# Five layers of message passing on a graph: one product's buffer doubled, its sums cut in two around a gather, and one addition placed earlier on VectorE

## The chip, the cores and the metric

The kernel runs on one core of one Trainium2 chip. The metric is the device time of one execution in microseconds (us), median of several runs; lower is better.

## What is computed

The graph has 12,500 nodes of 64 features and 200,000 edges of 32 features, sorted by their destination. The reference, cut to what matters:

```python
h = jnp.maximum(_layernorm(x), 0.0)
for l in range(5):
    h_ = _leaky(x @ W1[l] + b1[l]) @ W2[l] + b2[l]
    e = _leaky(edge_attr @ We1[l] + be1[l]) @ We2[l] + be2[l]
    msg = h_[src] * e * dot_scale[l]
    agg = jax.ops.segment_sum(msg, dst, num_segments=n)
    out = x + agg * res_w[l]
    x = layernorm(out) * ln_g[l] + ln_b[l]
return x_input + x
```

(Inside the loop `x` is the state that starts as `h`.)

## The kernel before

All values are 32-bit floats. The state of all nodes lies in SBUF, features on partitions 0 to 63 (`nodes_state`). The rows `h_[src]` come from a table in HBM (`h_rows`) that each layer writes. The edges are split in two kinds.

**Slot edges.** The first 101,376 edges in the order of the destinations, in 9 chunks, were sorted by source in a prologue into 126 groups of 1,024 slots, 14 per chunk, so that the 112 source rows of a group are contiguous in the table. They are loaded by plain DMAs and spread to the slots by a product with a one-hot matrix (`gathered`, line 1053). **Window edges.** The other 97 groups of 1,024 edges have their source rows gathered by indirect DMAs on GpSimd (line 793), 8 per group, into a ring of 9 buffers; one more group holds the spilled edges of the chunks. 92 of these 98 groups are spread over the 126 steps of a layer's loop (so about three steps in four have one; `a_at(s)` is None in the others), and 6 follow in six tail steps.

One loop step `s` works on three groups at different depths. The order on each engine is written out by hand in `step` and is this (in brackets: only where that step has a window group, or where a tile of nodes is due):

- TensorE: [hidden layer of window group s+2], hidden layer of slot group s+2 (line 976), [second layer of window group s+1], second layer of slot group s+1 (line 980), [window sums of s, line 1016], **chunk sums** of s (`chunk_sums`, line 1029: 32 products of 64x64 by 64 x width in four quadrants of the array), [a part of a node tile, "middle"], the slot gather of s+1 (line 1053), [a part of a node tile, "end"].
- VectorE: [window product of s: gathered rows times edge values, line 1750], **slot product** of s (line 1757), [one-hot matrix of the next window group, line 1670, 640 elements], leaky ReLU of s+2 for both kinds (line 1662), bias of the slot edges of s+1 then of the window edges of s+1 (line 1666), ["middle"], the **one-hot matrix of the slots** of s+1 (line 1670, 8 x width elements), [**window additions**: two additions of the window sums of s into the state, line 1718, with two register loads of their column, line 1782], [at a chunk's end: four additions of the chunk's sums, line 1731, with two register loads of their own, line 1724], ["end"].
- ScalarE: a tenth of the hidden values of s+2 (line 1241), and parts of node tiles.

The chunk's width is the number of destination columns: 360, 328, 288, 248, 208, 168, 128, 88 and 48 in the nine chunks. Hidden values and sums of window groups share one PSUM bank (`win_ps` is `hid_ps[0]`). So TensorE's hidden layer of s+3 waits in step s+1 until all additions of step s are done (`added`, in `step` of TensorE). The second layer of window group s+1 overwrites `e_ps`, so it waits for the window product of s; the second layer of the slots waits for the slot product, the gather for the slots' bias. There is one buffer for slot products, so the slot product of s waits until the chunk sums of s-1 are done (`sum_ready`). When the sums of all nodes of a tile are final, the tile's normalization and the next layer's node network are done in fixed places of nine steps in a row: centering and variance on TensorE at the "end" of the first two, reciprocal (line 1604) in the "middle" of the third step on VectorE. The variance also uses the shared bank and waits for the same step's window additions. Up to twelve places for tiles lie in the loop, two in the six tail steps; the rest of the tiles follows.

## Time and profile before

| what | value |
|---|---|
| median of 3 runs | 6610.09 us (6605.63 to 6611.65) |
| the profiled execution | 6615.82 us |
| span of its profile | 6614.0 us |
| TensorE matmul busy | 5622.6 us, 85% of the span |
| VectorE busy | 5148.4 us, 78% |
| GpSimd busy | 4527.2 us, 68% |
| ScalarE busy | 1133.9 us, 17% |
| moved by DMA | 886.20 MB, 134 GB/s in the mean |

The first 1,250 us are the sorting prologue. Then come five layers. In each the 126 steps take about 980 us (from the first slot product to the last: 987.2, 984.0, 979.4, 987.7 and 941.7 us), and the tail, the remaining nodes and the start of the next layer about 105 us. An engine's busy share is a mean over steps in which another one may be the limit; so the waits inside a step say more. In lists of waits "A <- B: us, times, longest" means that A's queue stood still until B had finished. A wait on "issue" is time in which the profile shows nothing that the engine waited for: its sequencer was busy with register loads or branches, which are no busy time.

### The profile page before, as it was taken

Reading aid. Unit: us, or ns where it says so; the run is one execution under the profiler, and the core shown is the slowest. Engines: PE = TensorE matmul, PEld = TensorE weight load, DVE = VectorE, ACT = ScalarE, POOL = GpSimd, SP = SyncE. Lnnn points to the kernel's source line nnn. Section 1 sums busy time; section 2 is a strip of 40 time slices with the busy share of each in tenths; the row PEclk is TensorE's granted clock in tenths of the full one; section 3 lists DMA queues with packets and bytes.
Section 4 is the critical chain, followed back from the end, with each engine's and each line's share of the span. In section 5 each row is a group of like instructions: output and inputs, shape, how many; then the busy total and the mean of one; then the engine's idle time right before and its main releaser. Section 6 shows DMA issues by size and latency. Waiting matters only on the chain.

```text
span 6614.0 us, 169076 instructions
## 1 busy us (share of the span) xinstructions
PE 5622.6 (85%) x63332; PEld 3676.7 (56%) x63333; DVE 5148.4 (78%) x7991; ACT 1133.9 (17%) x1726; POOL 4527.2 (68%) x4793
## 2 busy tenths in 40 slices
PE   6776899988888788888878888888898887888887
PEld 2223444456666555666655666655566665556665
DVE  8997544688887688888768888867888875888886
ACT  0000211111122211112211112221111222111111
POOL 5777777666677377777727777746777773777775
PEclk9997555799999799999979999988999997999998
DMA  3112399755566355656635655644565563666664
GB/s 135 26 26 47 78 240 242 185 131 138 138 148 152 96 132 136 142 141 154 159 80 133 145 143 143 162 112 116 129 147 142 148 161 78 139 147 156 151 171 110
DMA packets 733545, 886.20 MB, mean 134 GB/s; under 512 B 325488, under 2 KB 502976, under 8 KB 731568
## 3 DMA queue, kind: packets, MB, share of 16 engines
q1 hardware_dynamic: 568480, 703.64, 40.8%
q0 software_dynamic: 152144, 154.93, 12.4%
q10 hardware_dynamic: 12096, 16.53, 0.8%
q8 instruction: 530, 8.68, 0.6%
q14 instruction: 295, 2.42, 0.1%
HBM read 749.51 MB, written 125.06 MB: 132 GB/s over the span
## 4 chain that ended last, share of the span: by engine, by line
PE 54%; DVE 21%; issue 15%; DVEq 4%; ACT 3%; DMA 1%; POOL 0%; ACTq 0%; SPq 0%; POOLq 0%
PE bank L980 14%; PE bank L976 8%; PE bank L1029 7%; PE bank L1053 5%; PE bank L922 4%; PE bank L879 3%; DVE arena L1662 3%; PE bank L1016 3%; PE bank L860 2%; PE bank L845 2%; DVEq L1782 2%; DVE arena L1750 2%; ACT arena L1241 2%; DVE arena L1670 2%; DVE arena L1408 2%
## 5 line engine op out<-in xcount | busy, mean ns | idle before, releaser
L793 POOL DMA_INDIRECT arena<-h_rows,src x3855 | 3674.3, 953 | 1693.5 <-issue 1250.7
L980 PEld LDWEIGHTS bank<-w2s,arena 128*128 128x128 f32 x8960 | 1175.7, 210 | 772.3 <-DVE arena L1750 437.2
L980 PE MATMUL bank<-w2s,arena 128*128 128x128 f32 x8960 | 1307.0, 303 | 208.2 <-DVE arena L1750 191.4
L780 POOL DMA_INDIRECT slots<-arena,slot_index x792 | 787.2, 994 | 267.2 <-issue 241.3
L976 PE MATMUL bank<-nodes_state,edge_w 64*128 64x512 f32 x980 | 598.4, 693 | 307.3 <-DVE nodes_state L1718 142.6
L1053 PEld LDWEIGHTS bank<-arena 112*64 112x64 f32 x20160 | 640.4, 138 | 267.0 <-issue 245.1
L1053 PE MATMUL bank<-arena 112*64 112x64 f32 x20160 | 725.8, 225 | 60.1 <-issue 54.2
L976 PE MATMUL bank<-x_packed,edge_w 64*128 64x512 f32 x1260 | 740.1, 669 | 16.4 <-ACT std L1190 15.6
L1241 ACT ACTIVATE arena<-bank,tenth 128x512 f32<-128x512 f32 x490 | 335.5, 685 | 2296.6 <-PE bank L976 2296.6
L1662 DVE SCALAR_TENSOR_TENSOR arena<-bank,edge_w,arena 128x512 f32<-128x512 f32 x490 | 366.7, 748 | 424.1 <-ACT arena L1241 421.4
L1670 DVE TENSOR_TENSOR x_packed<-bank,slot_rel 128x2880 f32<-128x2880 f32 (+8 forms) x315 | 588.9, 1870 | 15.8 <-issue 15.8
L1670 DVE TENSOR_TENSOR arena<-bank,slot_rel 128x2880 f32<-128x2880 f32 (+8 forms) x315 | 588.6, 1869 | 12.5 <-issue 12.5
L1666 DVE TENSOR_TENSOR arena<-bank,b2s 128x512 f32<-128x512 f32 x630 | 432.4, 686 | 157.4 <-PE bank L980 153.7
L1241 ACT ACTIVATE x_packed<-bank,tenth 128x512 f32<-128x512 f32 x630 | 430.0, 683 | 680.0 <-PE bank L976 680.0
L1029 PE MATMUL bank<-x_packed,arena 64*64 64x288 f32 (+8 forms) x10080 | 524.3, 346 | 0.0
L1029 PE MATMUL bank<-arena 64*64 64x288 f32 (+8 forms) x10080 | 523.9, 346 | 0.0
L1662 DVE SCALAR_TENSOR_TENSOR arena<-bank,edge_w,x_packed 128x512 f32<-128x512 f32 x630 | 467.6, 742 | 59.5 <-ACT x_packed L1241 51.7
L1757 DVE TENSOR_TENSOR arena<-arena,bank 128x512 f32<-128x512 f32 x630 | 429.4, 682 | 43.8 <-PE bank L1053 39.1
L1016 PE MATMUL bank<-arena 128*64 128x80 f32 x7760 | 411.3, 253 | 42.4 <-DVE arena L1662 35.4
L1016 PEld LDWEIGHTS bank<-arena 128*64 128x64 f32 x7760 | 328.4, 148 | 122.3 <-DVE arena L1662 60.4
L1670 DVE TENSOR_TENSOR arena<-bank,rel 128x640 f32<-128x640 f32 x485 | 396.1, 817 | 0.0
L1029 PEld LDWEIGHTS bank<-x_packed,arena 64*64 64x64 f32 x10080 | 311.1, 135 | 127.8 <-issue 6.5
(198 smaller groups left out, 5615.6 us busy)
## 6 DMA issues: line engine op xcount, KB each, us to landing
arena<-slot_pick SPq DMA_DIRECT2D x630, 448.0 KB
arena<-h_rows SPq DMA_DIRECT2D x630, 224.0 KB
x_packed<-slot_attr SPq DMA_DIRECT2D x630, 128.0 KB
nodes_state<-attr_t SPq DMA_DIRECT2D x485, 128.0 KB
arena<-h_rows,src POOLq DMA_INDIRECT x3855
slot_pick<-arena SPq DMA_DIRECT2D x126, 448.0 KB
x_packed<-slots SPq DMA_DIRECT2D x127, 136.0 KB, 4.9
slots<-arena SPq DMA_DIRECT2D x9, 1904.0 KB, 22.1
```

The lines of the kernel that those rows point to most:

```text
L780: pool.indirect_dma_start(slots, bass.IndirectOffsetOnAxis(ap=slot_index[:, t:t + 1], axis=0), records[:, v, j, :], None).then_inc(record_ ...
L793: pool.indirect_dma_start(to[0:n, at:at + D], None, table, bass.IndirectOffsetOnAxis(ap=index[0:n, t:t + 1], axis=0)).then_inc(landed(t), 16)
L976: return pe.matmul(hid_ps[k][:, :], edge_w[rows_of, 0:P], attributes, start=True, stop=True)
L980: mm = pe.matmul(to[:, j * P:(j + 1) * P], acts[:, j * TILE:(j + 1) * TILE], w2s[:, :], start=True, stop=True)
L1016: mm = pe.matmul(win_ps[side * D:(side + 1) * D, 0:WIN], msg[:, 0, at:at + D], pick[:, k % 2, side * TPH + j, :], start=(j == 0), stop=(j ...
L1029: mm = pe.matmul(sum_ps[half][side * D:(side + 1) * D, 0:w], msg[slots_of, 1, at:at + D], slot_places[i % 2][slots_of, k * w:(k + 1) * w], ...
L1053: mm = pe.matmul(slot_ps[half * D:(half + 1) * D, k * D:(k + 1) * D], source_pick[0:ROWS, i % 2, slot:slot + D], source_rows[0:ROWS, i % 2 ...
L1241: return act.activation(hid_tenth[k], hid_ps[k][:, :], ACT.Identity, scale=SLOPE, bias=tenth[:, :])
L1662: return dve.scalar_tensor_tensor(out, hid_ps[k][:, :], edge_w[:, 2 * P + D:2 * P + D + 1], hid_tenth[k], ALU.add, ALU.max)
L1666: return dve.tensor_tensor(out.rearrange("p (t f) -> p t f", f=D), of.rearrange("p (t f) -> p t f", f=D), b2s[:, :].unsqueeze(1).to_broadc ...
L1670: return dve.tensor_tensor(out, column_ps[:, 0:n].unsqueeze(1).to_broadcast((P, tiles, n)), where.unsqueeze(2).to_broadcast((P, tiles, n)) ...
L1757: dve.tensor_tensor(msg[:, 1, :], slot_e, slot_ps[:, :], ALU.mult).then_inc(slot_msg_ready, 1)
```

## The change

Three things are changed.

1. The slot products get two buffers, taken in turn (`slot_msg`). The second lies in a free part of `x_packed`. The wait ahead of the slot product goes; a wait for the chunk sums of an earlier group stands now ahead of the slots' one-hot matrix.
2. The chunk sums are made in two calls of 16 products each: the first stands where all 32 stood, the second behind the slot gather. The products with the spilled edges at a chunk's end follow the second.
3. On VectorE the window additions with their register loads stand ahead of the "middle" part and ahead of the slots' one-hot matrix. The chunk's additions keep their place at the end.

```diff
+        slot_msg = [msg[:, 1, :], late["msg"]]
...
-                def chunk_sums(i):
+                def chunk_sums(i, begin, end):
...
-                    for j in range(TPH):
+                    for j in range(begin, end):
...
-                                mm = pe.matmul(sum_ps[half][side * D:(side + 1) * D, 0:w], msg[slots_of, 1, at:at + D],
+                                mm = pe.matmul(sum_ps[half][side * D:(side + 1) * D, 0:w], slot_msg[i % 2][slots_of, at:at + D],
...
-                    if ends_chunk(i):
+                    if ends_chunk(i) and end == TPH:
...
-                        chunk_sums(s)
+                        chunk_sums(s, 0, TPH // 2)
                     part("middle")
                     if k is not None:
                         pe.wait_ge(slot_e_biased, l * NB + k + 1)
                         gathered(k)
+                    if b_at(s) is not None:
+                        chunk_sums(s, TPH // 2, TPH)
...
-                        if i > 0:
-                            dve.wait_ge(sum_ready, 4 * (l * (NB + CHUNKS) + i + i // BG))
-                        dve.tensor_tensor(msg[:, 1, :], slot_e, slot_ps[:, :], ALU.mult).then_inc(slot_msg_ready, 1)
+                        dve.tensor_tensor(slot_msg[i % 2], slot_e, slot_ps[:, :], ALU.mult).then_inc(slot_msg_ready, 1)
...
+                    if k is not None and k != SPILL_AT:
+                        group = GB0 + real(k)
+                        window_start[:] = [dve.value_load(start_i[0:1, 2 * group + side:2 * group + side + 1],
+                                                          min_val=0, max_val=NPAD) for side in range(2)]
+                        window_added(s, k)
                     part("middle")
                     if i is not None:
                         w = widths[i // BG]
+                        if i > 1:
+                            dve.wait_ge(sum_ready, 4 * (l * (NB + CHUNKS) + i - 1 + (i - 1) // BG))
                         one_hot(slot_places[i % 2][:, 0:TPG * w].rearrange("p (t w) -> p t w", w=w), TPG, w,
                                 slot_rel[:, i * TPG:(i + 1) * TPG])
...
-                    if k is not None and k != SPILL_AT:
-                        group = GB0 + real(k)
-                        window_start[:] = [dve.value_load(start_i[0:1, 2 * group + side:2 * group + side + 1],
-                                                          min_val=0, max_val=NPAD) for side in range(2)]
-                        window_added(s, k)
                     if ends_chunk(s):
                         chunk_added(s)
```

What this does to the order of VectorE at a chunk's end (the first chunk, width 360; the next chunk's width is 328, so the slots' one-hot matrix has 2624 elements). TENSOR_LOAD is a register load, ISA and REGISTER_ALU are waits and register arithmetic. Before:

```order
L1666 TENSOR_TENSOR arena<-bank,b2s 128x512
L1670 TENSOR_TENSOR arena<-bank,slot_rel 128x2624
L1782 TENSOR_LOAD start_i
L1782 ISA x2
L1782 TENSOR_LOAD start_i
L1782 ISA x2
L1714 ISA
L1716 REGISTER_ALU
L1718 ISA
L1718 TENSOR_TENSOR nodes_state<-nodes_state,bank 64x80
L1716 REGISTER_ALU
```

After the second window addition come the chunk's two register loads and additions at once. In the changed kernel:

```order
L1669 TENSOR_TENSOR arena<-bank,b2s 128x512
L1774 TENSOR_LOAD start_i
L1774 ISA x2
L1774 TENSOR_LOAD start_i
L1774 ISA x2
...
L1721 TENSOR_TENSOR nodes_state<-nodes_state,bank 64x80
L1781 ISA
L1673 TENSOR_TENSOR arena<-bank,slot_rel 128x2624
L1727 TENSOR_LOAD chunk_start
L1727 ISA x2
L1727 TENSOR_LOAD chunk_start
```

The window's register loads and additions moved ahead of the one-hot matrix, and the matrix stands now between them and the chunk's register loads.

The same for TensorE in a step of the third chunk (width 288) that has a part of a node tile in its "middle" (line 860 before, 861 after). Before:

```order
L1016 MATMUL bank<-arena 64x80 x8
L1029 MATMUL bank<-arena 64x288 x16
L461 COMPARE_AND_BRANCH
L1128 ISA
L857 REGISTER_ALU
L860 MATMUL bank<-node_w,y_act 112x64 x8
L461 UNCONDITIONAL_BRANCH
L1053 MATMUL bank<-arena 64x64 x16
```

In the changed kernel:

```order
L1017 MATMUL bank<-arena 64x80 x8
L1030 MATMUL bank<-arena 64x288 x8
L462 COMPARE_AND_BRANCH
L1131 ISA
L858 REGISTER_ALU
L861 MATMUL bank<-node_w,y_act 112x64 x8
L462 UNCONDITIONAL_BRANCH
L1054 MATMUL bank<-arena 64x64 x16
L1030 MATMUL bank<-arena 64x288 x8
```

Half of the chunk sums (the program's count; in the profile each such product shows twice) stands behind the gather now. No instruction is added but one wait, and one goes.

## Rows read from the trace of the kernel before

**Rows 1.** The page: busy time, share of the span, instructions, by engine.

```profile
PE 5622.6 (85%) x63332; PEld 3676.7 (56%) x63333; DVE 5148.4 (78%) x7991; ACT 1133.9 (17%) x1726; POOL 4527.2 (68%) x4793
```

**Rows 2.** Third layer: us; busy PE, PEld, DVE, ACT, POOL; clock; DMA; GB/s.

```profile
3428.40:3541.00 112.60, 100.73 (x1296) 64.93 (x1296) 102.49 (x126) 14.15 (x22) 85.43 (x90) 0.98 0.62 141
...
4331.00:4407.80 76.80, 68.82 (x1145) 53.57 (x1145) 58.89 (x104) 16.02 (x24) 50.17 (x53) 0.96 0.65 164
...
4407.80:4513.40 105.60, 72.57 (x338) 45.22 (x338) 46.56 (x73) 22.78 (x35) 12.84 (x14) 0.58 0.15 39
```

**Rows 3.** Waits of the whole run: who waited for whom, us, times, longest.

```profile
DVE arena L1662 <- ACT arena L1241: 421.4, 346, 8.5
...
PE bank L980 <- DVE arena L1750: 191.4, 172, 3.5
...
PE bank L976 <- DVE nodes_state L1718: 142.6, 138, 4.8
```

**Rows 4.** VectorE in time, first chunk: start, duration, instruction, count, [idle before <- releaser].

```profile
3459.81 0.68 DVE L1750 TENSOR_TENSOR arena<-arena,bank 128x512 f32<-128x512 f32 x1
...
3461.00 0.81 DVE L1670 TENSOR_TENSOR arena<-bank,rel 128x640 f32<-128x640 f32 x1
...
3463.65 0.69 DVE L1666 TENSOR_TENSOR bank<-bank,b2s 128x512 f32<-128x512 f32 x1
3464.25 3.14 DVE L1670 TENSOR_TENSOR x_packed<-bank,slot_rel 128x2880 f32<-128x2880 f32 x1
3467.31 0.59 DVE L1718 TENSOR_TENSOR nodes_state<-nodes_state,bank 64x80 f32 x2
3467.93 0.69 DVE L1750 TENSOR_TENSOR arena<-arena,bank 128x512 f32<-128x512 f32 x1
...
3475.65 0.69 DVE L1750 TENSOR_TENSOR arena<-arena,bank 128x512 f32<-128x512 f32 x1
...
3506.23 0.69 DVE L1750 TENSOR_TENSOR arena<-arena,bank 128x512 f32<-128x512 f32 x1
...
3508.29 0.75 DVE L1662 SCALAR_TENSOR_TENSOR arena<-bank,edge_w,arena 128x512 f32<-128x512 f32 x1 [0.78 <-ACT arena L1241]
...
3513.90 0.69 DVE L1757 TENSOR_TENSOR arena<-arena,bank 128x512 f32<-128x512 f32 x1
...
3521.63 0.67 DVE L1750 TENSOR_TENSOR arena<-arena,bank 128x512 f32<-128x512 f32 x1
```

**Rows 5.** TensorE in time: two rows of the last chunk, three of the first.

```profile
3259.72 0.78 PE L1016 MATMUL bank<-arena 128*64 128x80 f32 x16
...
3260.42 0.68 PE L1029 MATMUL bank<-x_packed,arena 64*64 64x48 f32 x32
...
3463.23 2.65 PE L1029 MATMUL bank<-arena 64*64 64x360 f32 x32
3465.81 1.15 PE L1053 MATMUL bank<-arena 112*64 112x64 f32 x32
...
3514.11 0.66 PE L976 MATMUL bank<-nodes_state,edge_w 64*128 64x512 f32 x1 [0.58 <-DVE nodes_state L1718]
```

**Rows 6.** VectorE in time, last chunk: window additions behind a short one-hot matrix.

```profile
3272.07 0.56 DVE L1670 TENSOR_TENSOR arena<-bank,slot_rel 128x384 f32<-128x384 f32 x1 [0.45 <-issue]
...
3273.62 0.60 DVE L1718 TENSOR_TENSOR nodes_state<-nodes_state,bank 64x80 f32 x2 [0.99 <-issue]
```

**Rows 7.** Chunk's ends: what line 1731 waited for, and TensorE after one.

```profile
  issue: 42.9, 35
...
3034.20 1.19 PE L976 MATMUL bank<-nodes_state,edge_w 64*128 64x512 f32 x1 [5.66 <-DVE nodes_state L1731]
```

**Rows 8.** Line 838 (variance of a node tile, TensorE): what it waited for, us, times.

```profile
  DVE nodes_state L1718: 19.1, 36
```

**Rows 9.** TensorE in the tail: first product of the next layer's node network.

```profile
3349.56 1.11 PE L845 MATMUL bank<-nodes_state,node_w 64*128 x1 [4.25 <-ACT nodes_state L1275]
```

**Rows 10.** GpSimd in time: a layer's first gather, with the idle time before it.

```profile
3411.86 0.95 POOL L793 DMA_INDIRECT arena<-h_rows,src  x1 [100.66 <-issue]
```

More of the change, by code:

```diff
@@ L170, in build @@
         late, at = {}, 0
-        for name, n in dict(place=TPG * WMAX, tenth=HALF, attr=2 * HALF, x=TN, spill_pick=WMAX, spill_msg=HALF).items():
+        for name, n in dict(place=TPG * WMAX, tenth=HALF, attr=2 * HALF, x=TN, spill_pick=WMAX, spill_msg=HALF, msg=HALF).items():
             late[name] = x_packed[:, at:at + n]
```

## The prediction

> **What bounds the kernel now.** I read the page first, then stretches by chunk, then the list of waits, then single steps in time. By the page [rows 1] TensorE is busy 85% and VectorE 78%; neither is full. The stretches [rows 2] show why: in the widest chunk both are nearly full (TensorE 100.73 and VectorE 102.49 of 112.60 us), in the narrowest TensorE leads (68.82 against 58.89 of 76.80), and the tail is a chain in which nobody is full. So a step is set by the two engines handing work to each other, and the reader should look at the waits between them [rows 3]: VectorE stands 421.4 us before a leaky ReLU until ScalarE has its tenth, which only means that TensorE's hidden layer came late; TensorE stands 142.6 us before the hidden layer for the window additions, and 191.4 us before the second layer for the window product. A wait in one of these lists can be covered by the other engine's work, so I walk a few steps.
>
> A step of the widest chunk with all its parts runs on VectorE without a gap: window product to window product 8.12 us (3459.81 to 3467.93) [rows 4]. The next takes 7.72 us (to 3475.65). Where the following group is missing it takes 7.67 us (3506.23 to 3513.90), with 0.78 us idle before the leaky ReLU at 3508.29; and where its own window group is missing 7.73 us (3513.90 to 3521.63), although it has the least work. A turn of four steps with three window groups is therefore about 8.12 + 7.72 + 7.67 + 7.73 = 31.24 us. The idle time comes from TensorE's hidden layer, which starts only when the window additions are over: 0.58 us idle at 3514.11 [rows 5]. The additions stand behind a one-hot matrix of 3.06 us (start to next start) [rows 4]. That is the cycle which the change opens.
>
> **Part 1, the additions earlier.** They run now right behind the bias. The hidden layer then never waits for them in a wide chunk: TensorE has the chunk sums of 2.58 us (3463.23 to 3465.81) and the gather of 1.15 us [rows 5] to do before it gets there. What does not change is that the window product follows the one-hot matrix, and that the second layer waits for it; that wait (191.4 us) stays.
>
> What is new is the register loads. Where nothing covers them, the additions start 1.55 us after the instruction that went out before them: 3272.07 to 3273.62, 0.99 us of it idle [rows 6]. Before, the long one-hot matrix hid them. Now only the two biases of 0.60 us each stand ahead, and all leave together when the slots' second layer ends. So the exposed time is 1.55 - 1.20 = 0.3 us with both biases, 1.55 - 0.60 = 0.9 us with one, less what VectorE still has queued. The Trainium skill (Runtime: NRT & Kernel Launch, Instruction fetch mechanics) puts a register load at about 200 ns, so two would hide behind one bias and the 0.3 and 0.9 would be zero; by that the four-step turn below would gain another 0.95 us, some 50 us over the three widest chunks. Our row shows more, so I keep the row's price.
>
> The four steps again, by what each instruction takes of VectorE from its start to the next start: 0.60 us for a bias or a product, which is 0.09 under its duration; by the same measure 0.66 for a leaky ReLU and 0.73 for the small one-hot matrix (0.75 and 0.81 long); 3.06 for the slots' matrix and 0.62 for the two additions [rows 4]. All parts: 8.12, unchanged, since VectorE is some 0.6 us behind TensorE at the bias and that hides the loads. No window leaky ReLU: VectorE is on time at the bias, so the exposed 0.3 us shows, 8.12 - 0.66 + 0.3 = 7.8. No following window group, so neither small matrix nor second bias: 8.12 - 0.73 - 0.60 + 0.65 (0.9 less a backlog of 0.25) = 7.45. No own window group, so neither product, additions nor loads: 8.12 - 0.60 - 0.62 = 6.9. Together 30.3 against 31.24 us, or 0.23 us a step. Bounds: 0 (every exposure lands and the hidden layer's gain is eaten by the second layer's wait) to 0.4. I take 0.2 for the three widest chunks, 42 steps x 5 layers x 0.2 = **-42 us**; half for the next three, where one-hot matrix and chunk sums shrink alike but the exposure does not, **-21 us**; none for the last three.
>
> **Part 1 at a chunk's end.** Before, the chunk's register loads followed the additions directly: 42.9 us idle in 35 places [rows 7]. Now the one-hot matrix stands between and hides them. TensorE stands in front of the chunk's additions there (5.66 us in one case), so this is on the path. Most of it, **-35 us** (bounds -43 and -15, as the window's loads may be exposed instead).
>
> **Part 1 at node tiles.** The variance waited 19.1 us for window additions [rows 8]. Half of it, **-10 us** (bounds -19 and 0), since TensorE then waits for ScalarE's root in the same place. The reciprocal, 2.94 us, now stands behind the additions; in the loop it delays only the window product, as before. In the tail it is different: there TensorE's next hidden layer stands behind the first product of the node network, which waits (4.25 us) for the normalized tile [rows 9]. Additions and their loads push the tile back by 0.62 + 0.9 less what the reciprocal waited anyway: about 1.4 us, twice in each of four layers, **+11 us** (bounds 0 and 13).
>
> **Part 2, the sums in two halves.** Nothing is added to TensorE's work. The gather comes earlier by half the chunk sums, 1.3 us at width 360 and 0.3 us at 48 [rows 5]. Its cover while the slots' bias runs (0.67 us with its start) shrinks by the same. With window sums ahead (0.70 us, 3259.72 to 3260.42) that is enough. In a step without them the narrow chunks leave 0.3 to 0.65 us of cover: a stall up to 0.35 us in 27% of the 56 steps of four chunks in five layers is 76 x 0.35 = 27 us at most; the second half then covers VectorE, so I take **+10 us** (bounds 0 and 27). The hidden layer stands where it stood counted from the second layer, and the slot product is not among the long waits [rows 3], so an earlier gather gains nothing by itself. Next late is the window product.
>
> **Part 3, the second buffer.** The removed wait was always met, because the old sums were done before the gather on the same queue; 0. The new wait asks for sums two groups back; 0. Without the second buffer the slot product would have to wait for the second half: the buffer pays for part 2.
>
> Sum: -42 - 21 - 35 - 10 + 11 + 10 = -87 us. The profiled execution took 6615.8 us (span 6614.0, the rest around it), 5.7 above the median; I subtract from the median 6610.1: **6523 us**, given as 6520.
>
> **Rivals.**
> - *The register loads set the pace; slower.* Place: VectorE between bias and window additions, in every loop step with a window group: 91 a layer, 455 in all, 170 of them with one bias. Full price 170 x 0.9 + 285 x 0.3 = 239 us, against it the 142.6 us of the hidden layer's waits, the chunk's ends and the other terms (-35 - 10 + 21): about +72 us, **6680 us**. It decides when VectorE arrives at the bias without a backlog in most steps. For it: in the narrow chunks TensorE leads. Against: in the wide ones VectorE is the one behind.
> - *A wash.* The hidden layer's wait moves to the second layer's, and only the ends of chunks (-35), tiles (-10) and the costs (+21) stay: -24, and part of that lost, **6590 to 6610 us**.
> - *The clock.* After the 5.66 us gap TensorE's products took 1.19 us where the same took 0.66 at 3514.11 [rows 5, 7], so it had fallen from 2.4 to 1.2 GHz; the granted clock of the loops is 0.96 to 0.98 [rows 2], or 4 to 8% of the five loops' 4880 us at the lower level, about 300 us, in which half is lost. If shorter gaps keep it up half the time, another -75 us: **6445 us**. The Trainium skill (TensorE: Matmul & The Clock Gate, Part 1: The HAM clock gate) says that activity releases the throttle and idling sets it, which would favour this; the gap shrinks by a quarter only, so I doubt it.
> - *GpSimd.* It ends its gathers 100.66 us before the next layer's first one [rows 10], so it bounds nothing unless a layer's loop loses well over 60 us.
>
> That the change doesn't do what it says is no rival: the order shows the moves.
>
> **How the numbers follow.** My forecast (6520, own range 6480 to 6565) has 0.50; the clock 0.13; the wash 0.14; the register loads 0.20; something else 0.03. About 0.2% (13 us) is what a measurement can tell from no change. Faster: 0.50 + 0.13 + a part of the wash 0.05 = 0.68; same: 0.10; slower: 0.22. The range leaves out about half of the clock's case below and half of the slower case above: 6440 to 6680.
>
> **What would show it.** Right: the hidden layer's wait for line 1721 (was 1718) falls from 142.6 us to under 40; VectorE's wait before the leaky ReLU from 421 to under 350; "issue" before the chunk's additions from 42.9 to near 0, while "issue" before the window additions rises by 50 us or more; the first chunk of a layer falls from 112.6 us [rows 2] by about 3. Wrong: TensorE's wait for the window product above 300 us, or the gather waiting for the bias by more than 60 us, with the loop no shorter.

## The result and the profile after

| | before | after |
|---|---|---|
| median | 6610.87 us, 4 runs (6605.63 to 6620.89) | **6656.53 us**, 4 runs (6649.67 to 6663.22) |
| the profiled execution; its span | 6615.82; 6614.0 us | 6649.67; 6647.8 us |

The ratio is 1.0065, with a 95% interval of 1.0049 to 1.0081. So the change costs 46 us, where 87 us were to be gained: the sign of the forecast is wrong.

The page of the kernel after, busy time by engine, to be held against [rows 1]:

```profile
PE 5676.3 (85%) x63332; PEld 3617.7 (54%) x63333; DVE 5173.4 (78%) x7991; ACT 1136.4 (17%) x1726; POOL 4520.1 (68%) x4793
```

TensorE issues the same 63,332 products and is busy 53.7 us longer. The page's groups say where (columns: line, engine, operation, tiles, count, busy us, mean ns, idle before with its releaser). The chunk sums, line 1030 now:

```profile
L1030 PE MATMUL bank<-x_packed 64*64 64x288 f32 (+8 forms) x10080 | 597.0, 353 | 0.0
L1030 PE MATMUL bank<-arena 64*64 64x288 f32 (+8 forms) x10080 | 594.4, 351 | 0.0
...
L1721 DVE TENSOR_TENSOR nodes_state<-nodes_state,bank 64x80 f32 x970 | 227.4, 234 | 266.5 <-PE bank L1017 101.5
```

and the same lines of the kernel before:

```profile
L1029 PE MATMUL bank<-x_packed,arena 64*64 64x288 f32 (+8 forms) x10080 | 524.3, 346 | 0.0
L1029 PE MATMUL bank<-arena 64*64 64x288 f32 (+8 forms) x10080 | 523.9, 346 | 0.0
```

The same 20,160 products take 1191.4 us of busy time instead of 1048.2: 143 us more, although the mean of one product has hardly moved (353 and 351 ns against 346). A busy time counts overlapping products once; it grew because less of the stretch overlaps. Why is to be seen in single steps. TensorE in time, a step of the widest chunk, kernel after (start, us, line, tiles, count):

```profile
3467.01 0.77 PE L1017 MATMUL bank<-arena 128*64 128x80 f32 x16
3467.71 1.44 PE L1030 MATMUL bank<-arena 64*64 64x360 f32 x16
3469.08 1.15 PE L1054 MATMUL bank<-arena 112*64 112x64 f32 x32
3470.16 1.44 PE L1030 MATMUL bank<-arena 64*64 64x360 f32 x16
3471.53 1.12 PE L977 MATMUL bank<-x_packed,edge_w 64*128 64x512 f32 x2
```

and a step of the narrowest one:

```profile
3262.26 0.45 PE L1030 MATMUL bank<-x_packed 64*64 64x48 f32 x16
3262.64 1.15 PE L1054 MATMUL bank<-arena 112*64 112x64 f32 x32
3263.72 0.45 PE L1030 MATMUL bank<-x_packed 64*64 64x48 f32 x16
3264.10 1.12 PE L977 MATMUL bank<-x_packed,edge_w 64*128 64x512 f32 x2
```

Read the starts, not the durations. At width 360 the first half takes 3469.08 - 3467.71 = 1.37 us and the second 3471.53 - 3470.16 = 1.37, together 2.74; the whole took 2.58 in [rows 5]. At width 48 the halves take 0.38 each, together 0.76; the whole took 0.61 (3260.42 to the gather at 3261.03). The difference is nearly the same, 0.15 to 0.16 us, at a width that is 7.5 times smaller. So it is no work of the products but a fixed cost of each unbroken stretch of chunk sums, and the split makes two stretches of one. The medians over the steps at the full granted clock say the same:

| width | whole, 32 products | half, 16 products | two halves less the whole |
|---|---|---|---|
| 360 | 2.581 us | 1.371 | 0.161 |
| 208 | 1.568 | 0.864 | 0.160 |
| 128 | 1.034 | 0.598 | 0.162 |
| 88 | 0.767 | 0.464 | 0.161 |
| 48 | 0.612 | 0.378 | 0.144 |

With 0.155 us in each of the 126 steps of five layers, 630 steps, this is **98 us** of TensorE. (A layer's last step has no gather to split around; the 625 others with the medians of the table give 99 us.) I call it the run-out below; whether it is paid at the start or at the end of a stretch, the rows do not say. In the sums of line 1030 above, each stretch is also drawn 0.07 us longer than its start-to-start time; a second stretch adds that once more, 44 us, and 98 + 44 = 142 is the 143 us that these groups grew by. The gather itself takes 1.08 us to the next start in both kernels, whether the hidden layer or a half of the sums follows.

The third layer by stages, kernel after, for [rows 2] (us; busy PE, PEld, DVE, ACT, POOL; clock; DMA; GB/s); the second row covers the same twelve steps as there:

```profile
3432.30:3544.35 112.05, 101.47 (x1296) 62.77 (x1296) 102.71 (x126) 14.13 (x22) 84.75 (x90) 0.98 0.58 143
4347.60:4427.65 80.05, 70.29 (x1146) 54.25 (x1145) 60.04 (x104) 16.02 (x24) 45.84 (x49) 0.98 0.59 156
4427.65:4531.35 103.70, 66.92 (x338) 42.47 (x336) 46.69 (x74) 22.76 (x35) 12.19 (x13) 0.62 0.14 40
```

The widest chunk is 0.55 us shorter, where 3 us were expected, the narrowest is 3.25 us longer than its 76.80, and the tail is 1.9 us shorter.

The waits of the kernel after (who waited for whom, us, times, longest), against [rows 3]:

```profile
DVE arena L1665 <- ACT arena L1244: 327.4, 239, 8.3
...
PE bank L981 <- DVE arena L1753: 265.3, 199, 4.8
...
DVE nodes_state L1721 <- PE bank L1017: 101.5, 112, 4.0
DVE nodes_state L1721 <- issue: 88.8, 243, 1.1
...
PE bank L1054 <- DVE arena L1669: 27.1, 61, 1.0
...
PE bank L977 <- DVE nodes_state L1721: 2.8, 6, 1.0
```

The hidden layer's wait for the window additions is gone (142.6 to 2.8 us), as planned; the second layer's wait for the window product (now line 1753) went from 191.4 to 265.3, and VectorE stands 190 us ahead of the window additions (101.5 + 88.8), where it stood 64.5 (62.9 on issue and 1.6 for the window sums).

### The profile page after: what moved, and what is told of

Its sections match the earlier page's. It is cut to its first block, busy times and chain, and to the rows that moved or that the text cites. A ratio compares the mean times of both kernels' runs of the same rounds, so it can differ in the third digit from the quotient of the medians.

```text
span 6647.8 us, 169040 instructions
## 1 busy us (share of the span) xinstructions
PE 5676.3 (85%) x63332; PEld 3617.7 (54%) x63333; DVE 5173.4 (78%) x7991; ACT 1136.4 (17%) x1726; POOL 4520.1 (68%) x4793
## 4 chain that ended last, share of the span: by engine, by line
PE 54%; DVE 22%; issue 16%; DVEq 3%; ACT 3%; DMA 1%; POOL 0%; ACTq 0%; SPq 0%; POOLq 0%
PE bank L981 13%; PE bank L1030 8%; PE bank L977 6%; PE bank L1054 6%; PE bank L923 4%; DVE arena L1665 4%; PE bank L1017 3%; PE bank L880 3%; PE bank L846 2%; DVE arena L1753 2%; PE bank L861 2%; DVE arena L1411 2%; PE bank L902 2%; DVE arena L1669 2%; DVEq L1774 2%
## 5 line engine op out<-in xcount | busy, mean ns | idle before, releaser
L981 PEld LDWEIGHTS bank<-w2s,arena 128*128 128x128 f32 x8960 | 1160.3, 208 | 879.4 <-DVE arena L1753 518.2
L981 PE MATMUL bank<-w2s,arena 128*128 128x128 f32 x8960 | 1293.7, 300 | 324.9 <-DVE arena L1753 265.3
L1665 DVE SCALAR_TENSOR_TENSOR arena<-bank,edge_w,arena 128x512 f32<-128x512 f32 x490 | 366.4, 748 | 335.9 <-ACT arena L1244 327.4
L1030 PE MATMUL bank<-x_packed 64*64 64x288 f32 (+8 forms) x10080 | 597.0, 353 | 0.0
L1030 PE MATMUL bank<-arena 64*64 64x288 f32 (+8 forms) x10080 | 594.4, 351 | 0.0
L1721 DVE TENSOR_TENSOR nodes_state<-nodes_state,bank 64x80 f32 x970 | 227.4, 234 | 266.5 <-PE bank L1017 101.5
L1669 DVE TENSOR_TENSOR bank<-bank,b2s 128x512 f32<-128x512 f32 x490 | 338.5, 691 | 31.8 <-PE bank L981 31.7
```

What stands on the lines that cost most here:

```text
L981: mm = pe.matmul(to[:, j * P:(j + 1) * P], acts[:, j * TILE:(j + 1) * TILE], w2s[:, :], start=True, stop=True)
L1030: mm = pe.matmul(sum_ps[half][side * D:(side + 1) * D, 0:w], slot_msg[i % 2][slots_of, at:at + D], slot_places[i % 2][slots_of, k * w:(k + ...
L1665: return dve.scalar_tensor_tensor(out, hid_ps[k][:, :], edge_w[:, 2 * P + D:2 * P + D + 1], hid_tenth[k], ALU.add, ALU.max)
L1669: return dve.tensor_tensor(out.rearrange("p (t f) -> p t f", f=D), of.rearrange("p (t f) -> p t f", f=D), b2s[:, :].unsqueeze(1).to_broadc ...
```

## The experiments

Theory T after the result: the split's second run-out costs about 98 us of TensorE a run, and it is on the path, since TensorE's idle time cannot take it up. Theories R and P as rivals: the register loads, uncovered now, eat what the moved additions give (R; the expectations call it L); the second half's place, behind the gather, costs (P). The first four kernels undo one part at a time; they and the kernel before (6616.76 us) ran on one chip.

**e1: the split and the second buffer, the additions where they stood.** The kernel after with this edit:

```diff
@@ VectorE, ahead of part("middle")
-                    if k is not None and k != SPILL_AT:
-                        group = GB0 + real(k)
-                        window_start[:] = [...]
-                        window_added(s, k)
@@ behind the slots' one-hot matrices
+                    if k is not None and k != SPILL_AT:
+                        group = GB0 + real(k)
+                        window_start[:] = [...]
+                        window_added(s, k)
```

> The chunk sums in two halves around the gather and the second buffer, as in the change; the window additions stand where they stood before. Theory T (the split costs TensorE time): after the change each half of the sums occupies TensorE for 1.37 us at width 360, together 2.74, where the whole took 2.58; at width 48 0.38 + 0.37 us where the whole took 0.61. That is 0.14 to 0.16 us in each of 630 steps, up to 95 us. T expects this kernel to be slower than before by 30 to 95 us, most of it in the two narrowest chunks. Theory L (the register loads, now uncovered behind the biases, set the pace and the split is free): this kernel within 10 us of before.

Measured 6701.98 us, ratio 1.0132 [1.0114, 1.0149]: **+85 us**. The split with its buffer costs more than the whole change. That is in T's range and refutes L's "within 10 us". T's "most of it in the two narrowest chunks" missed: from slot product to slot product, over the five layers, the two narrowest chunks lost 28 of the 74 us that the loops lost.

**e2: the additions alone.** The kernel before with the same lines moved the other way, one buffer, sums whole.

> Only the window additions with their register loads ahead of the middle part and the slots' one-hot matrix; the sums whole, one buffer. Theory L: slower than before by 30 to 60 us, VectorE standing some 190 us before the window additions as in the changed kernel (101.5 + 88.8 us). Theory T: faster than before by 10 to 60 us, since the hidden layer's 142.6 us of waits go, the chunk's register loads are hidden (42.9 us) and TensorE keeps whole sums.

Measured 6545.28 us, ratio 0.9894 [0.9877, 0.9911]: **-71 us**, against L, and 11 us more than T allowed for. The sums are back at 2.58 us. TensorE in time, e2 (lines as in the kernel before):

```profile
3401.97 2.65 PE L1029 MATMUL bank<-x_packed,arena 64*64 64x360 f32 x32
3404.55 1.15 PE L1053 MATMUL bank<-arena 112*64 112x64 f32 x32
```

So the change holds a part that gains 71 us and a part that loses more. Its waits for the window product and ahead of the additions:

```profile
PE bank L980 <- DVE arena L1750: 337.8, 274, 4.8
...
DVE nodes_state L1718 <- PE bank L1016: 119.1, 129, 4.0
...
DVE nodes_state L1718 <- issue: 81.0, 228, 1.4
```

**e3: e2 with the window's two register loads early.** They go out behind the small one-hot matrix, two leaky ReLUs and two biases ahead of their use:

```diff
                         one_hot(pick[:, m % 2, :, :], TPG, WIN, rel[:, at:at + TPG])
+                    if k is not None and k != SPILL_AT:
+                        group = GB0 + real(k)
+                        window_start[:] = [...]
...
                         edge_biased(e_ps[:, :], e_ps[:, :]).then_inc(e_biased, 1)
                     if k is not None and k != SPILL_AT:
-                        group = GB0 + real(k)
-                        window_start[:] = [...]
                         window_added(s, k)
```

> As the one before, with the window's two register loads issued behind the small one-hot matrix at the start of the step, and only the additions left behind the biases. Theory L: 40 us or more faster than the kernel with the moved additions alone, the waits before the additions gone (under 30 us). Theory T: the loads matter too but less, 0 to 30 us faster than that kernel.

Measured **6468.36 us**, ratio 0.9776 [0.9760, 0.9791]: 77 us under e2 and 148 us under the kernel before. It is the fastest of all. L's expectation (40 us or more) holds here, and T's (0 to 30 us) missed. VectorE in time, kernel after, a step with one bias ahead of the additions:

```profile
3483.03 0.69 DVE L1669 TENSOR_TENSOR arena<-bank,b2s 128x512 f32<-128x512 f32 x1
3484.58 0.60 DVE L1721 TENSOR_TENSOR nodes_state<-nodes_state,bank 64x80 f32 x2 [0.86 <-PE bank L1017]
```

with TensorE's window sums of the same step,

```profile
3482.92 0.78 PE L1017 MATMUL bank<-arena 128*64 128x80 f32 x16
```

and e3, a step of the same kind:

```profile
3411.30 0.68 DVE L1666 TENSOR_TENSOR arena<-bank,b2s 128x512 f32<-128x512 f32 x1
3412.15 0.60 DVE L1718 TENSOR_TENSOR nodes_state<-nodes_state,bank 64x80 f32 x2 [0.17 <-PE bank L1016]
```

Bias to additions is 1.55 us in the one, the very figure of [rows 6], and 0.85 in the other. In both cases the trace books the wait to TensorE's window sums; in the first these had ended at 3482.92 + 0.78 = 3483.70, 0.88 us before the additions, so what came last must have been the register loads. The queue's own rows of the loads in the kernel after (duration in ns: least, median, most):

```profile
L1774 DVEq TENSOR_LOAD <-start_i x970: 296/303/691, 1247.6 to 6632.3; - x194
L1774 DVEq FUSED_REGOPS  x970: 183/190/211, 1248.0 to 6632.6; - x194
```

Two loads with their register operations are 2 x (0.303 + 0.190) = 0.99 us, out of the 1.55. The Trainium skill (Runtime: NRT & Kernel Launch, Instruction fetch mechanics) gives about 200 ns for each register of a TENSOR_LOAD, for loads from HBM; by that figure two would hide behind one bias. These loads read SBUF, and the rows (303 ns, and 190 ns of register operations behind each) and the 77 us do not agree with it.

In e3 no wait of the additions is booked to "issue" for more than 1.8 us in all:

```profile
PE bank L980 <- DVE arena L1750: 274.2, 240, 4.7
...
DVE nodes_state L1718 <- PE bank L1016: 63.2, 99, 4.0
...
DVE nodes_state L1718 <- issue: 1.8, 6, 0.5
```

**e4: the kernel after with the loads early in the same way.**

> The changed kernel with the window's register loads issued early, everything else as changed. Theory L: back to the time of before or faster (at most 6600 us). Theory T: 0 to 30 us faster than the changed kernel and still slower than before by 10 us or more.

Measured 6581.26 us, ratio 0.9949 [0.9934, 0.9964]: 75 us under the kernel after, by the medians, and **113 us over e3**, which differs from it by the split and the second buffer alone. Here too T's expectation missed (75 us and not 0 to 30, and the time is below the kernel before), and L's "at most 6600 us" held. So the change has two costs, and neither theory alone gives all four results: the uncovered loads cost some 75 us with or without the split, the split costs 85 to 113 us with the loads hidden or not. Only the split makes the change slower than the kernel before; with the loads exposed and no split (e2) it is 71 us faster. TensorE's gather waits a little more for the bias in it than in e3 (its row there was 5.0 us):

```profile
PE bank L1054 <- DVE arena L1669: 22.3, 49, 1.0
```

**Where the time is, by TensorE.** The trace cut to the five loops, first slot product to last, adds up to these lines (us, then busy time by engine); one for each kernel, before, after, e1, e2, e3 and e4:

```profile
sum 4880.02, PE 4296.11 PEld 3070.71 DVE 4078.34 ACT 897.58 POOL 3571.19; mean PE 859.22 PEld 614.14 DVE 815.67 ACT 179.52 POOL 714.24
```
```profile
sum 4919.67, PE 4360.38 PEld 3012.41 DVE 4100.74 ACT 901.48 POOL 3575.91; mean PE 872.08 PEld 602.48 DVE 820.15 ACT 180.30 POOL 715.18
```
```profile
sum 4953.52, PE 4401.10 PEld 3040.78 DVE 4077.69 ACT 897.40 POOL 3583.81; mean PE 880.22 PEld 608.16 DVE 815.54 ACT 179.48 POOL 716.76
```
```profile
sum 4810.98, PE 4232.03 PEld 3024.68 DVE 4096.60 ACT 900.71 POOL 3565.00; mean PE 846.41 PEld 604.94 DVE 819.32 ACT 180.14 POOL 713.00
```
```profile
sum 4731.67, PE 4222.78 PEld 3020.84 DVE 4083.25 ACT 900.29 POOL 3541.73; mean PE 844.56 PEld 604.17 DVE 816.65 ACT 180.06 POOL 708.35
```
```profile
sum 4846.42, PE 4342.78 PEld 2997.89 DVE 4076.67 ACT 901.29 POOL 3565.43; mean PE 868.56 PEld 599.58 DVE 815.33 ACT 180.26 POOL 713.09
```

Loop time less TensorE's busy time is its idle time there. The busy time can be parted once more with the clock records of the trace: what falls at 1.2 GHz counts half as work, and the other half is what the lower clock cost. In those loops TensorE's granted clock was at 1.2 GHz for 476 us in the kernel before, 436 in the one after, 470, 399, 374 and 393 in e1 to e4. From that, per part:

| step | loops | work | lower clock | idle |
|---|---|---|---|---|
| move the additions (before to e2) | -69 | -21 | -43 | -5 |
| loads early (e2 to e3) | -79 | -5 | -5 | -70 |
| split (e3 to e4) | +115 | +103 | +17 | -5 |
| split (e2 to after) | +109 | +101 | +27 | -20 |
| split (before to e1) | +74 | +102 | +3 | -32 |

The split adds 101 to 103 us of work in all three pairs, whatever stands around it, and the run-outs by the starts are 98. From e3 to e4 it adds 34, 33 and 36 us in the three widest, the middle and the three narrowest chunks, the same at every width. That is T. How much of it shows in the time differs: where VectorE is still the late one, TensorE's idle time gives a part back (32 us in e1), and the clock adds some (22 of the 64 us that the three narrowest chunks of e4 lost against e3).

The first row is a surprise: moving the additions left the idle time alone and shortened the busy time. Two lines carry 50 of the 64 us (21 + 43), the hidden layer (1338.5 us in the kernel before, all forms, 1311.9 in e2) and the second layer (1307.0 and 1283.2), with unchanged counts.

In the first layer's loop the granted clock rose from 0.95 to 0.97, in the others by 0.01 or not at all. The rows of that loop (start and end of the stretch, us, busy times, clock), before and e2:

```profile
1247.43:2234.62 987.19, 869.84 (x11929) 622.03 (x11929) 818.67 (x1145) 185.28 (x279) 677.12 (x710) 0.95 0.59 143
```
```profile
1246.08:2208.94 962.86, 846.95 (x11929) 605.04 (x11930) 821.80 (x1146) 186.74 (x281) 677.62 (x710) 0.97 0.60 147
```

By the clock records 100 us of that loop were at 1.2 GHz before and 69 in e2. So 43 of the 69 us that the move gained in the loops came as clock. Why the clock rose while the idle time stayed was not tried, and what the other 21 us of work are is not resolved.

**Where the sums stand (P).** Four more kernels: e5, the kernel before with the second buffer and its moved wait alone; e6, all chunk sums in one go behind the gather (16 calls in the code, each of which is two products in the trace, so the 32 of the rows); e7, three quarters ahead and a quarter behind; e8, e3 with the node tile's three register loads at the start of the step.

```diff
 e5:                     chunk_sums(s, 0, TPH)            # ahead of the gather, additions in their old place
 e6:                     gathered(k)
                         chunk_sums(s, 0, TPH)            # behind it
 e7:                     chunk_sums(s, 0, TPH - 1)
                         gathered(k)
                         chunk_sums(s, TPH - 1, TPH)
 e8 (on e3):
-                    if sub == 0 and at == "middle":
-                        now[0] = slot(s)
...
+                if sub == 0 and tile_parts:
+                    now[0] = slot(s)
                 step(i, part)
```

> Only the second buffer for slot products, with the wait for the sums moved to the one-hot matrix; the sums whole and ahead of the gather, the window additions where they stood before. Every theory expects no difference from before (within 10 us): the removed wait was always met. If this kernel is slower by 30 us or more, the loss of the split kernel (85 us) lies in the buffer or the new wait and not in the split.

> The changed kernel with all 16 chunk sums of a step in one call behind the gather. Theory T (each call has a run-out of its own, so two calls cost 0.15 us of TensorE a step): TensorE's busy time falls by 70 to 140 us to near 5550, and the time comes to 6545 to 6600 us, near the kernel with the moved additions alone. Theory P (the sums cost time because they stand behind the gather and hold up the next hidden layer, or uncover the gather's wait for the bias): slower than the changed kernel, 6680 us or more, as twice as much stands behind.

> The changed kernel with three quarters of the chunk sums ahead of the gather and one quarter behind. Theory T: two calls as in the changed kernel, so TensorE's busy time as there (5660 to 5690 us) and the time within 20 us of it (6635 to 6675). Theory P: half of what stands behind is gone, so about half of the split's loss (111 us against the kernel with the moved additions alone) comes back: 6590 to 6615 us.

> The fastest so far (additions moved, window's register loads early, sums whole) with the three register loads of a place for a node tile at the start of its step instead of its middle, on all engines. TensorE stands 55 us before the gather and VectorE 89 us before the one-hot matrix on issue there. Theory L in the form that fits so far (an exposed register load costs about what it shows, where VectorE and TensorE take turns): 30 to 80 us faster than that kernel (6390 to 6440 us). If exposed loads are mostly covered by the other engine: within 15 us of it (6455 to 6480).

In all of their runs the kernel before itself took 11,251 to 11,281 us, so their ratios hold for that condition only. It does not belong to certain chips: one of the four (number 13) is the chip on which the kernel before took 6616.76 us beside e1 to e4 an hour earlier. The expectations of the repeats, which met the same condition:

> The kernel with only the second buffer again, on a chip where the kernel before takes its 6610 us. Every theory expects no difference from before (within 10 us). If it is slower by 30 us or more, the loss of the split kernel (85 us) lies in the buffer or the new wait and not in the split.

> All 16 chunk sums of a step in one call behind the gather, again. Theory T (each call has a run-out of its own): TensorE's busy time near 5550 us, the time 6545 to 6600 us. Theory P (what stands behind the gather costs time): slower than the changed kernel, 6680 us or more. Where the kernel before took 11281 us this one was the slowest of four (ratio 1.036), which speaks for P.

> Three quarters of the sums ahead of the gather, one quarter behind, again. Theory T: within 20 us of the changed kernel (6635 to 6675), TensorE's busy time 5660 to 5690. Theory P: half of the split's loss comes back, 6590 to 6615 us.

> The moved additions with early register loads and whole sums (6468 us), and the node tile's three register loads at the start of their step, again. If an exposed load costs about what it shows: 6390 to 6440 us. If the other engine covers it: 6455 to 6480 us.

> All 16 chunk sums of a step in one call behind the gather, otherwise as changed. Theory T (two calls cost 0.155 us of TensorE a step, 98 us in all): TensorE's busy time near 5550 us, the time 6545 to 6600 us. Theory P (what stands behind the gather costs time): slower than the changed kernel, 6680 us or more.

> Three quarters of the sums ahead of the gather, one quarter behind, otherwise as changed. Theory T: still two calls, so within 20 us of the changed kernel (6635 to 6675). Theory P: half of the split's loss of 111 us comes back, 6590 to 6615 us.

> The moved additions with early register loads and whole sums (6468 us), and the node tile's three register loads at the start of their step on all engines. If an exposed load costs about what it shows: 6390 to 6440 us. If the other engine covers it: 6455 to 6480 us.

> All 16 chunk sums of a step in one call behind the gather, otherwise as changed. Theory T alone (the second call's run-out, 98 us, is all of the loss): TensorE's busy time near 5550 us, the time 6545 to 6570 us. T with a share of P (the gather uncovered, the hidden layer behind the sums): 6570 to 6650 us. Theory P alone: slower than the changed kernel, 6680 us or more.

> The changed kernel with all 16 chunk sums behind the gather in one go, so one run-out a step and no second one. Run-out alone (the split costs its 98 us of extra run-outs, the place costs nothing): the time of the kernel that only moves the additions, 6545 us, a ratio of 0.99. If the place behind the gather costs too (the gather comes up to 2.6 us early, before the slots' bias, and TensorE stands): 6640 us or more, a ratio over 1.00.

> The fastest version with the node tile's three register loads at the step's start too. 90 node tiles are added in the loops behind register loads; if these are exposed as the window's were, some 0.5 to 1 us each in the steps that have one, it gains 0 to 40 us on the 6468 us: ratio 0.972 to 0.978. If they are hidden beside the bias already, it stays at 0.978, or loses some 20 us by standing in front of the small one-hot matrix's successors: 0.981.

| kernel | medians, us | ratios to before beside it |
|---|---|---|
| e5, buffer only | 11258.91, 11251.31 | 0.9976 [0.9952, 1.0000], 0.9991 |
| e6, sums behind | 11689.54, 11667.79, 11658.14, 11673.82, 11648.29 | 1.0363, 1.0356, 1.0335, 1.0353, 1.0356 [1.0314, 1.0398] |
| e7, three quarters ahead | 11470.64, 11498.81, 11468.21 | 1.0173 [1.0143, 1.0203], 1.0198, 1.0170 |
| e8, tile loads early | 11305.39, 11326.22, 11304.16, 11301.39 | 1.0033, 1.0048, 1.0034, 1.0021 [0.9998, 1.0043] |

What can be taken from them is little. The second buffer by itself costs nothing (e5); at 6610 us it was not tried alone, but the split's work there, 101 to 103 us with the buffer, is hardly more than the run-outs. The place behind the gather costs: e6 has one run-out a step, as the kernel before, and still loses 3.6%; the run-out alone (T) does not explain it. Two waits differ. Where the sums stand last, TensorE's gather waits 501.5 us for the slots' bias (46.0 us in e5), and its waits on "issue", large in both, stand more ahead of the sums than of the gather. From the page and the waits of e6 in its last run:

```profile
L1054 PE MATMUL bank<-arena 112*64 112x64 f32 x20160 | 904.0, 240 | 841.4 <-DVE arena L1667 501.5
```
```profile
PE bank L1030 <- issue: 896.9, 1556, 2.4
```

and of e5, where they stand more ahead of the gather (847.2 us, and 433.1 ahead of the sums):

```profile
PE bank L1054 <- issue: 847.2, 1202, 2.5
```

Such ratios do not carry over to 6610 us. e8 holds e3 in it, which gains 2.2% there, and is 0.2 to 0.5% slower than the kernel before here.

Where the kernel before takes 6610 us, what P costs beside T **stays open**, and so does whether e8 would improve on e3. The table by parts bounds P: from e3 to e4 TensorE stands 35 us more ahead of the gather (60.5 to 95.4) and 58 us less ahead of the second layer (331.8 to 273.5), and its idle time in the loops does not grow. The measured 113 us do not need P: 103 of work, 17 of clock and -5 of idle time are the 115 of the loops. Whether the clock's part comes from the place was not tried.

## Why the prediction was wrong

**The step that failed is part 2.** It said "Nothing is added to TensorE's work", priced the split at +10 us and bounded it by 0 and 27. It measured +85 us by itself (e1) and +113 us beside the moved additions (e4 against e3). What was added is no product but the fixed cost of a second 64x64 stretch, 0.155 us, 630 times. The cost that part 2 did name came as priced: the gather's wait for the slots' bias rose from 5.7 to 16.0 us in e1, +10 us (27.1 in the kernel after). The term put at nothing was the larger one. The rows for it were at hand: the chunk sums of [rows 5] take 2.58 us at width 360 and 0.61 us at width 48. Per column that is (2.58 - 0.61) / 312 = 0.0063 us, so 48 columns should take 0.30 us and 0.31 us are left that no width explains. A constant of 0.31 us in a call that is about to be cut in two needs a price between 0 and 0.31 us x 630 = 195 us. With widths that lie on one line the rest is nearer to the truth: 128 and 360 columns (1.034 and 2.581 us) leave 1.034 - 128 x 0.00667 = 0.18 us, and the 0.767 us at 88 columns fits the same line; 48 columns take 0.11 us more than it. The halves leave 0.17 us, so nearly all of the rest belongs to the stretch. The Trainium skill (TensorEngine Tiling (Array Packing), Key Properties) says that changing the tiling mode, not merely the tile, drains TensorE. The rows agree in kind: the sums in 64x64 stand between the window sums (128x64), the gather (112 rows, 64 columns) and the hidden layer (64x128), and the split adds one such change. That the drain is this constant was not tested. The page gives no figure, and the prediction did not weigh it, though it speaks against this change.

**The moved additions: right in sign, too large, by another path.** Their terms were -42 - 21 - 35 - 10 + 11 = -97 us; e2 measured -71. They came in other places than said. The steps were to gain 42 us in the three widest chunks, 21 in the middle three and nothing in the last; with the chunks' ends the loops of e2 gained 9, 55 and 5 us, and 40 of the 55 are clock. The step that failed in the widest chunks is the backlog that was to hide the register loads: e3, which hides them, gains another 47 us there. In e2 the first chunk of the third layer took 110.80 us against 112.60, where about 3 us were expected. At the chunks' ends (-35) "issue" ahead of the chunk's additions fell from 42.9 to 4.7 us in e2 (2.7 in the kernel after), but TensorE's wait for these additions fell only from 75.4 to 62.2; and in the kernel after 27.0 us of the additions' wait came back, booked to TensorE's spill sums, line 1044, which stand behind the gather there. At node tiles (-10) the variance's wait of 19.1 us went whole.

Of the named signs, the hidden layer's wait fell as said (142.6 to 2.8 us in the kernel after, under 40), and so did the wait before the leaky ReLU (327.4, under 350). "issue" before the window additions rose from 62.9 to 88.8 us, 26 and not 50 or more; the rest of their new wait, 1.6 to 101.5 us, is booked to the window sums, and 46 us of that go away with the loads in e4.

**The tail, +11 us, came as a wait.** The wait of 4.25 us in [rows 9] is 5.94 us in the kernel after, twice in each of four layers: 13.5 us in all (38.7 to 52.2 us, and the same in e2). The stage is no longer for it: [rows 2] has 105.60 us at a clock of 0.58, the kernel after 103.70 at 0.62, e2 104.85 at 0.61.

**The rivals.** *Register loads:* the price was real, since hiding them gave 77 and 75 us, a third of the "full price" of 239; that they would make the kernel slower was wrong, e2 is faster with them exposed. The measured time, 6656.53, is near this rival's 6680, but for another reason; that is luck. *The clock:* held to be unlikely, and it is the larger part of what the move gained, 43 of the 75 us that it was priced at. The prediction read 0.96 to 0.98 and about 300 us at 1.2 GHz from three stretches; over the whole loops it was 0.95 to 0.96, and 476 us. *The wash* and *GpSimd* did not show; GpSimd's busy time is 4520.1 us against 4527.2. *The second buffer* at 0: e5 agrees, under its condition.

**A sign that misled.** A wait for the window product above 300 us was named as a sign of failure. It stands at 337.8 us in e2, which is 71 us faster than before, and at 265.3 us in the kernel after, which is slower. A wait grows when the engine arrives sooner; only beside the busy time and the length of the stretch does it say who won.

## What to carry to other kernels

Before a stretch of products is cut in two, take its start-to-start time at three widths, keep those that lie on one line, and ask what is left at width zero: that rest may be paid again for every piece (here 0.18 us, of which 0.16 was). When instructions are moved towards the front of a step, move what feeds them (register loads) further still, ahead of work that covers them. And test the parts of a combined change apart: here one part was worth 71 us, with its loads early 148, and the other cost 113.

## What the runs showed of the hardware

- Each unbroken stretch of packed 64x64 products carries a fixed cost of 0.144 to 0.162 us of TensorE, at widths from 48 to 360 columns. The gather, 1.08 us to the next start, does not depend on what follows it. From 88 to 360 columns the stretch's time is a line in the width; at 48 columns it is 0.11 us above that line.
- A register load from SBUF takes VectorE's queue 303 ns, and 190 ns of register operations follow. Two of them hold the next instruction back until 1.55 us after the one that went out before them, and the trace may book that to a semaphore that was long given (3483.70 against 3484.58).
- TensorE's clock rose in the loops (0.95 to 0.97 in the first layer, 476 to 399 us at 1.2 GHz over all five) when waits were only moved, with 584 and 579 us of idle time in all; two thirds of the busy time saved were the clock's.
- The same program can take 11,270 us, 1.7 times as long, at a granted clock of 0.71, also on a chip that ran it in 6617 us an hour before. GpSimd then waits 4,040 us for its source indices, where it waited 143.4 us. The cause is not known. The rows, kernel before in its usual time and e5 in this condition:

```profile
  DMA src<-src_tiles: 143.4, 89
```
```profile
  DMA src<-src_tiles: 4040.4, 381
```
